# Self-attention of a decoder stack: the softmax is normalised by GpSimd before the transposes, without the matmuls that spread the inverse sums

## The chip, the cores and the metric

One core of a Trainium2 chip runs the whole program. Its engines are TensorE (matmuls and transposes, PE in the rows; PEld are its weight loads), VectorE (DVE), ScalarE (ACT), GpSimd (POOL) and SyncE (SP, which issues DMAs). The metric is the time of the device in microseconds, from the first to the last instruction and what lies around it, the median of several runs.

## The reference, cut to what matters

Two batches of 1024 tokens with 256 features go through two decoder layers. The change is in the first part of all, a self-attention of 16 heads of 64 features with a bias that depends on the distance of two tokens:

```python
x = x + attention(layernorm(x), Wq, Wkv, Wo, bo, rel_emb)      # x: (2, 1024, 256)
# inside, per batch and head:
q, k, v = ...                              # (1024, 64) each
s = q @ k.T * 64 ** -0.5 + bias(rel_emb)   # (1024, 1024)
p = softmax(s, axis=-1)
o = p @ v
```

A cross-attention and a mixture of experts, two attentions within groups, another cross-attention and a low-rank mixture follow. They take the rest of the time and are the same in both kernels.

## The kernel before, in words

The function `self_attention` works through 8 pairs of heads, for each of them through 2 batches, and within these through 8 tiles of 128 queries: 128 iterations n, each with two heads (0 and 1, side by side in the 64-row halves of TensorE). A tile of one head is numbered st = 2n + head; there are 256. For one tile:

- TensorE makes 128x1024 scores in two PSUM banks (L577; a product of float32 is made of three of the rounded parts and their remainders).
- VectorE's `biased` (L734) adds the bias strip, writes the negated sum to one of four buffers `sm` and keeps the row minimum.
- ScalarE's `exps` (L662) makes the exponentials in place and, by its accumulator, their row sums in `rsum`.
- TensorE's `transposed` (L590) turns the 128x1024 exponentials in two halves of four transposes, in two PSUM banks. ScalarE's `emptied` (L667) copies the first bank to `pT`, VectorE's `emptied` (L741) the second.

Two iterations share 256 query columns; such a couple is g = n // 2. One couple later TensorE's `values` (L605) multiplies `pT` by V, one half of the keys in an even iteration and the other in an odd one, into the left half of bank 6. After the second half it makes the **spread** (L612): four small products, each of the inverse sums of one tile, repeated over 64 columns, with the identity. They lay the inverse sum of every query over the 64 rows of its head in the right half of bank 6. ScalarE's `spread_inverse` (L673) copies that half to `inv`, VectorE's `normed` (L752) multiplies the left half by it into `o`, and SyncE stores `o`. VectorE's `inverted` (L746) takes the reciprocal of the four sums of a couple before. So the exponentials are transposed unnormalised, and the output is normalised.

Between these, each of the first 120 iterations projects one unit of the next block's k, q or v (TensorE L628 to L636; ScalarE L683 to L689; VectorE L761 to L768): four units of k and q, then four of v, in turn. The last 8 iterations project nothing.

Each engine runs its own queue in the order in which it is written, and semaphores order the engines: an instruction waits until a count is reached. TensorE's order in iteration n is: scores of n + 1; transposes of head 0 of n; half of the value products of the couple before, with the spread in every second iteration; transposes of head 1 of n; projection. `Signals.zero` (L69 to L71) has GpSimd clear the semaphores of a stage that is over, one instruction for each; in the self-attention that is all that GpSimd does.

Of the kernel before, what the change touches and what calls it, by code (L numbers as in the profile page):

```python
# [28 lines left out]
P = 128  # L29
# [447 lines left out]
def self_attention(nc, A, S, K, psum, early):  # L477
# [6 lines left out]
    with ExitStack() as ctx:  # L484
# [17 lines left out]
        inv = sb("inv", [P, GQ])  # L502
# [25 lines left out]
        with nc.Block() as block:  # L528
# [35 lines left out]
            def _(pe):  # L564
# [17 lines left out]
                def transposed(n, hl):  # L582
                    st = 2 * n + hl
                    pe.wait_ge(sig("exps"), st + 1)
# [8 lines left out]
                def values(g, half):  # L593
# [8 lines left out]
                    for kt in range(half * KT // 2, (half + 1) * KT // 2):  # L602
                        for hl in range(2):
                            rows = slice(hl * DH, (hl + 1) * DH)
                            pe.matmul(bank_o[rows, 0:GQ], V[:, b, kt, rows], pT[:, g % 2, hl, kt, :],  # L605
                                      start=kt == 0, stop=kt == KT - 1)
                    if half:
                        pe.wait_ge(sig("inverse"), g + 1)
                        for t in range(2):
                            for hl in range(2):  # L610
                                at = (4 * g + 2 * t + hl) % SUMS
                                last = pe.matmul(bank_o[hl * DH:(hl + 1) * DH, GQ + t * P:GQ + (t + 1) * P],  # L612
                                                 rsum[:, at:at + 1].broadcast_to([P, DH]), ident[:, :], start=True, stop=True)
# [42 lines left out]
            def _(a):  # L656
                def exps(st):
                    a.wait_ge(sig("biased"), st + 1)
                    at = st % SUMS
                    if st >= SUMS:  # L660
                        a.wait_ge(sig("o_ps"), st // 4 - 2)
# [40 lines left out]
                for n in range(NI):  # L702
                    if n % 2 == 0 and n > 2:
                        spread_inverse(n // 2 - 2)
# [10 lines left out]
                spread_inverse(NG - 2)  # L715
                spread_inverse(NG - 1)

            @block.gpsimd
            def _(g):
                for signals in old:  # L720
                    signals.zero(g)

            @block.vector
            def _(v):
# [18 lines left out]
                def inverted(g):  # L743
                    v.wait_ge(sig("exps"), 4 * (g + 1))
                    part = rsum[:, 4 * g % SUMS:4 * g % SUMS + 4]
                    v.reciprocal(part, part).then_inc(sig("inverse"), 1)  # L746
# [1631 lines left out]
```

## Time and profile before

| | before |
|---|---|
| median of 3 runs | 2372.37 us (2369.58 to 2373.74) |
| the profiled execution | 2370.43 us, its span 2368.7 us |
| granted TensorE clock, mean of the span | 0.943 |
| TensorE busy | 2102.1 us (89% of the span) |
| its weight loads | 1733.0 us (73%) |
| VectorE busy | 1471.8 us (62%) |
| ScalarE busy | 1031.8 us (44%) |
| GpSimd busy | 605.0 us (26%) |
| self-attention's loop | from 54 to 929 us, about |

Busy shares are means over stages with different limits. The page also cuts the span into 40 slices of 59 us: the self-attention is roughly slices 2 to 16, in which TensorE is busy for nine tenths or more, and GpSimd for nothing. Whether an engine waits, and for whom, is read from the timeline and the list of waits. Ends of matmuls are modelled; the starts of weight loads are the firmer mark.

### The profile page before, as it was taken

How to read it: one execution, taken by the hardware profiler on the slowest of the kernel's cores; microseconds unless marked ns; L12 is line 12 of the kernel's file. 1: busy time of each engine (PE TensorE's matmuls, PEld its weight loads, DVE VectorE, ACT ScalarE, POOL GpSimd, SP SyncE). 2: the span in 40 equal slices, each digit the busy share in tenths (PEclk: the TensorE clock that was granted, in tenths of full speed). 3: DMA queues.
4: the chain of work that ended last, by engine and by line, in shares of the span. 5: the costliest groups of instructions: out<-in, count | busy, mean ns of one | idle time of the engine just before them, and what ended most of it. 6: DMA issues, size and time to landing. Idle time of an engine off the chain costs nothing. (4 is left out here: it accounts for less than half of the span.)

```text
span 2368.7 us, 54589 instructions
## 1 busy us (share of the span) xinstructions
PE 2102.1 (89%) x22556; PEld 1733.0 (73%) x22556; DVE 1471.8 (62%) x3140; ACT 1031.8 (44%) x2036; POOL 605.0 (26%) x594
## 2 busy tenths in 40 slices
PE   6999999999999998788887579999868999958885
PEld 4777777777777776667775468999858999956773
DVE  6666666666666664489889645555435454525885
ACT  3666656665666663234333233424224243313442
POOL 1000000000000000166666613343302433424552
PEclk9999999999999999899998779999979999979996
DMA  7001111010101012111200030000021000002000
GB/s 247 15 10 52 43 59 46 17 43 16 46 17 43 12 38 93 56 37 38 65 19 10 18 131 15 12 20 12 11 98 52 29 16 29 12 29 97 10 10 19
DMA packets 59991, 97.17 MB, mean 41 GB/s; under 512 B 7720, under 2 KB 50480, under 8 KB 57392
## 3 DMA queue, kind: packets, MB, share of 16 engines
q1 hardware_dynamic: 53760, 71.98, 9.3%
q10 hardware_dynamic: 5984, 21.69, 2.3%
q8 instruction: 180, 2.95, 0.5%
q14 instruction: 67, 0.55, 0.1%
HBM read 70.45 MB, written 23.20 MB: 40 GB/s over the span
## 5 line engine op out<-in xcount | busy, mean ns | idle before, releaser
L734 DVE CUSTOM_DVE_ANT_0 a_sm<-psum,a_strip 128x1024 f32<-128x1024 f32 x256 | 311.8, 1218 | 33.1 <-PE psum L577 33.1
L662 ACT ACTIVATE a_sm<-a_sm,a_mn 128x1024 f32<-128x1024 f32 x256 | 293.4, 1146 | 29.5 <-DVE a_mn L734 29.4
L667 ACT ACTIVATE a_pT<-psum 128x512 f32<-128x512 f32 x256 | 152.8, 597 | 302.6 <-PE psum L590 302.6
L590 PE MATMUL psum<-ident,a_sm 128*128 128x128 f32 x2048 | 280.0, 280 | 1.1 <-ACT a_pT L667 1.0
L590 PEld LDWEIGHTS psum<-ident,a_sm 128*128 128x128 f32 x2048 | 219.8, 141 | 83.6 <-issue 57.5
L741 DVE COPY a_pT<-psum 128x512 f32<-128x512 f32 x256 | 176.3, 689 | 131.7 <-PE psum L590 131.7
L605 PE MATMUL psum<-a_pT,a_V 128*64 128x256 f32 x2048 | 249.0, 385 | 1.3 <-DVE a_o L752 1.3
L1150 POOL TENSOR_TENSOR b_x_in<-b_x_in,b_bo_a 128x512 f32<-128x512 f32 x8 | 10.2, 1277 | 911.0 <-POOLq L528 911.0
L605 PEld LDWEIGHTS psum<-a_pT,a_V 128*64 128x64 f32 x2048 | 135.7, 136 | 77.7 <-issue 22.1
L1038 PE MATMUL psum<-b_w,b_act_hi 128*128 128x256 f32 x256 | 64.7, 337 | 59.3 <-POOL b_act_lo L1138 59.3
L577 PE MATMUL psum<-a_KH,a_QH 64*128 64x512 f32 x512 | 114.6, 443 | 2.5 <-DVE a_mn L734 2.5
L1146 POOL TENSOR_TENSOR b_gs<-b_gate,b_sg 128x512 f32<-128x512 f32 x64 | 96.6, 1509 | 30.3 <-ACT b_sg L1062 29.8
L577 PE MATMUL psum<-a_KL,a_QH 64*128 64x512 f32 x512 | 101.8, 392 | 0.0
L577 PE MATMUL psum<-a_KH,a_QL 64*128 64x512 f32 x512 | 101.2, 390 | 0.0
L219 PE MATMUL psum<-sa_eT,sa_wqkv 128*128 128x256 f32 x768 | 97.4, 286 | 2.7 <-DVE sa_eT L1777 2.7
L219 PE MATMUL psum<-la_eT,la_wqkv 128*128 128x256 f32 x768 | 97.9, 287 | 1.7 <-DVE la_eT L1777 1.7
L1038 PEld LDWEIGHTS psum<-b_w,b_act_hi 128*128 128x128 f32 x256 | 44.8, 212 | 71.9 <-POOL b_act_lo L1138 70.5
L219 PEld LDWEIGHTS psum<-sa_eT,sa_wqkv 128*128 128x128 f32 x768 | 94.4, 194 | 3.4 <-DVE sa_eT L1777 3.1
L219 PEld LDWEIGHTS psum<-la_eT,la_wqkv 128*128 128x128 f32 x768 | 94.9, 195 | 2.4 <-DVE la_eT L1777 2.1
L1138 POOL TENSOR_TENSOR b_act_lo<-b_act,b_act_hi 128x512 fp32r<-128x512 f32 x64 | 81.7, 1278 | 54.5 <-ACT b_act_hi L1069 54.5
L628 PE MATMUL psum<-a_hT_hi,a_W 128*128 128x512 f32 x256 | 76.5, 421 | 6.8 <-PEq L318 6.8
L1062 ACT ACTIVATE b_sg<-b_gate 128x512 f32<-128x512 f32 x64 | 40.4, 631 | 92.2 <-DVE b_gate L1215 92.0
(379 smaller groups left out, 4584.8 us busy)
## 6 DMA issues: line engine op xcount, KB each, us to landing
a_strip<-table SPq DMA_DIRECT2D x16, 960.0 KB, 6.7
oT<-a_o SPq DMA_DIRECT2D x64, 128.0 KB, 1.9
b_oT_in<-oT SPq DMA_DIRECT2D x8, 1024.0 KB, 5.5
a_raw<-in_a_wqkv SPq DMA_DIRECT2D x7, 384.0 KB, 3.4
s_x<-in_x_rev SPq DMA_DIRECT2D x4, 512.0 KB, 7.5
vb<-s_zero SPq DMA_DIRECT2D x8, 256.0 KB, 2.9
b_x_in<-in_x SPq DMA_DIRECT2D x8, 256.0 KB, 5.6
b_vb_in<-vb SPq DMA_DIRECT2D x8, 256.0 KB, 5.6
```

Of the source, the lines that this page charges most:

```text
L219: last = pe.matmul(bank[:, i * CP:(i + 1) * CP], weight[:, wp, k, m * P:(m + 1) * P], cols[:, cp, k, :], start=n == 0, stop=n == len(terms ...
L577: last = pe.matmul(scores_banks(hl)[:, c, :], qq[rows, b, q], kk[rows, b, k], start=i == 0, stop=i == 2)
L590: last = pe.transpose(psum[:, 4 + j, k * P:(k + 1) * P], sm[:, st % RING, kt * P:(kt + 1) * P], ident[:, :])
L605: pe.matmul(bank_o[rows, 0:GQ], V[:, b, kt, rows], pT[:, g % 2, hl, kt, :], start=kt == 0, stop=kt == KT - 1)
L628: last = pe.matmul(bank, W[:, ws, k, col], hT[hs][:, k, tok], start=i == 0, stop=i == len(terms) - 1)
L662: a.activation(sm[:, st % RING, :], sm[:, st % RING, :], ACT.Exp, scale=-1.0, bias=mn[:, at:at + 1], accum_out=rsum[:, at:at + 1]).then_in ...
L667: a.activation(probs(st, 0), psum[:, 4, :].rearrange("p (k q) -> p k q", k=4), ACT.Copy).then_inc(sig("pT_act"), 1)
L734: v.tensor_tensor_reduce(out=sm[:, st % RING, :], in0=scores_banks(hl).rearrange("p c n -> p (c n)"), in1=strip[:, pair % 2, hl, qt * P:qt ...
L741: v.tensor_copy(probs(st, 1), psum[:, 5, :].rearrange("p (k q) -> p k q", k=4)).then_inc(sig("pT_dve"), 1)
L1038: last = pe.matmul(bank[:, t * D:(t + 1) * D], half[:, e % 2, k, t * P:(t + 1) * P], w2[:, e, k, :], start=i == 0, stop=i == len(parts) - 1)
L1138: g.tensor_tensor(act_lo[:, e % 2, :, :], act[:, e % 2, :, :], act_hi[:, e % 2, :, :].bitcast(F32), ALU.subtract).then_inc(sig("m_lo"), 1)
L1146: g.tensor_tensor(gs[:, n % ER, :, :], gate[:, n % ER, :, :], sg[:, n % ER, :, :], ALU.mult).then_inc(sig("m_gs"), 1)
```

## The change

GpSimd gets work in the self-attention. As soon as the exponentials of a tile and their row sums are there, VectorE takes the reciprocal of that tile's sums (`inverted`, now once a tile), and GpSimd multiplies the whole 128x1024 tile by it, in place (`scaled`), with the reciprocal broadcast along the row as the second operand. TensorE transposes the tile after that. So the exponentials are normalised before they are transposed, and the value products give the output itself: the spread, the copy of it and VectorE's product are gone, and ScalarE copies the output from PSUM to `o` (`stored`). GpSimd clears the old semaphores after its third product.

```diff
                 def transposed(n, hl):
                     st = 2 * n + hl
-                    pe.wait_ge(sig("exps"), st + 1)
+                    pe.wait_ge(sig("scaled"), st + 1)
...
                     if half:
-                        pe.wait_ge(sig("inverse"), g + 1)
-                        for t in range(2):
-                            for hl in range(2):
-                                at = (4 * g + 2 * t + hl) % SUMS
-                                last = pe.matmul(bank_o[hl * DH:(hl + 1) * DH, GQ + t * P:GQ + (t + 1) * P],
-                                                 rsum[:, at:at + 1].broadcast_to([P, DH]), ident[:, :], start=True, stop=True)
                         last.then_inc(sig("o_ps"), 1)
...
-                def spread_inverse(g):
+                def stored(g):
                     a.wait_ge(sig("o_ps"), g + 1)
-                    if g:
-                        a.wait_ge(sig("o_out"), g)
-                    a.activation(inv[:, :], bank_o[:, GQ:2 * GQ], ACT.Copy).then_inc(sig("inv_out"), 1)
+                    if g >= 2:
+                        a.wait_ge(sig(f"st{g % 2}"), 16 * (g // 2))
+                    a.activation(o[:, g % 2, :], bank_o[:, 0:GQ], ACT.Copy).then_inc(sig("o_out"), 1)
...
             def _(g):
-                for signals in old:
-                    signals.zero(g)
+                def scaled(st):
+                    at = st % SUMS
+                    g.wait_ge(sig("inverse"), st + 1)
+                    g.tensor_tensor(sm[:, st % RING, :], sm[:, st % RING, :], rsum[:, at:at + 1].broadcast_to([P, T]),
+                                    ALU.mult).then_inc(sig("scaled"), 1)
+
+                for st in range(2 * NI):
+                    scaled(st)
+                    if st == 2:
+                        for signals in old:
+                            signals.zero(g)
...
-                def normed(g):
-                    v.wait_ge(sig("inv_out"), g + 1)
-                    if g >= 2:
-                        v.wait_ge(sig(f"st{g % 2}"), 16 * (g // 2))
-                    v.tensor_tensor(o[:, g % 2, :], bank_o[:, 0:GQ], inv[:, :], ALU.mult).then_inc(sig("o_out"), 1)
+                def inverted(st):
+                    v.wait_ge(sig("exps"), st + 1)
+                    at = st % SUMS
+                    v.reciprocal(rsum[:, at:at + 1], rsum[:, at:at + 1]).then_inc(sig("inverse"), 1)
...
+                inverted(0)
                 for n in range(NI):
-                    if n % 2 == 0 and n > 2:
-                        normed(n // 2 - 2)
+                    inverted(2 * n + 1)
                     if n and NU + n - 1 < len(units):
                         project(NU + n - 1)
...
                         biased(2 * n + 3)
+                        inverted(2 * n + 2)
                     emptied(2 * n + 1)
-                    if n % 2:
-                        inverted(n // 2)
```

TensorE's queue in an iteration with a spread, from the transposes of head 0 to the next scores, before:

```order
L590 MATMUL psum<-ident,a_sm 128x128 x8
L605 MATMUL psum<-a_pT,a_V 64x256 x8
L612 MATMUL psum<-ident,a_rsum 64x128 x4
L590 MATMUL psum<-ident,a_sm 128x128 x8
L628 MATMUL psum<-a_hT_hi,a_W 128x512 x4
L628 MATMUL psum<-a_hT_lo,a_W 128x512 x2
L577 MATMUL psum<-a_KH,a_QH 128x512 x2
```

and now:

```order
L589 MATMUL psum<-ident,a_sm 128x128 x8
L604 MATMUL psum<-a_pT,a_V 64x256 x8
L589 MATMUL psum<-ident,a_sm 128x128 x8
L621 MATMUL psum<-a_hT_hi,a_W 128x512 x4
L621 MATMUL psum<-a_hT_lo,a_W 128x512 x2
L576 MATMUL psum<-a_KH,a_QH 128x512 x2
```

The spread's four products (L612) are gone; all else stands as it stood.

VectorE's queue from the second half of a projection of k to that of the next one, before (L734 is the bias operation, L761 the projection's second half):

```order
L761 TENSOR_TENSOR a_KL<-psum,a_KH 128x512
L734 ISA a_sm,a_mn<-psum,a_strip 128x1024
L734 ISA a_mn 128x1
L741 COPY a_pT<-psum 128x4x128
L734 ISA a_sm,a_mn<-psum,a_strip 128x1024
L734 ISA a_mn 128x1
L741 COPY a_pT<-psum 128x4x128
L746 RECIPROCAL a_rsum<-a_rsum 128x4
L752 TENSOR_TENSOR a_o<-psum,a_inv 128x256
L761 TENSOR_TENSOR a_KL<-psum,a_KH 128x512
```

and now (L736 is the bias operation, L757 the projection's second half):

```order
L748 RECIPROCAL a_rsum<-a_rsum 128x1
L757 TENSOR_TENSOR a_KL<-psum,a_KH 128x512
L736 ISA a_sm,a_mn<-psum,a_strip 128x1024
L736 ISA a_mn 128x1
L743 COPY a_pT<-psum 128x4x128
L736 ISA a_sm,a_mn<-psum,a_strip 128x1024
L736 ISA a_mn 128x1
L748 RECIPROCAL a_rsum<-a_rsum 128x1
L743 COPY a_pT<-psum 128x4x128
L748 RECIPROCAL a_rsum<-a_rsum 128x1
L757 TENSOR_TENSOR a_KL<-psum,a_KH 128x512
```

The product into `o` and the reciprocal of four sums are gone; a reciprocal of one tile's sums stands ahead of the projection's half and another ahead of the iteration's second copy.

GpSimd's queue where the self-attention begins, before (L71 clears a semaphore, L1150 belongs to the stage after):

```order
L360 MEMSET s_zero 128x512
L318 UNCONDITIONAL_BRANCH
L718 UNCONDITIONAL_BRANCH
L71 ISA x49
L528 UNCONDITIONAL_BRANCH
L1133 UNCONDITIONAL_BRANCH
L1150 TENSOR_TENSOR b_x_in<-b_x_in,b_bo_a 128x512
```

and now:

```order
L360 MEMSET s_zero 128x512
L318 UNCONDITIONAL_BRANCH
L711 UNCONDITIONAL_BRANCH
L716 TENSOR_TENSOR a_sm<-a_sm,a_rsum 128x1024 x3
L71 ISA x49
L716 TENSOR_TENSOR a_sm<-a_sm,a_rsum 128x1024 x253
L527 UNCONDITIONAL_BRANCH
L1126 UNCONDITIONAL_BRANCH
L1143 TENSOR_TENSOR b_x_in<-b_x_in,b_bo_a 128x512
```

The clearing stood first and alone; now it stands behind three products, and 253 follow it.

## Rows read from the trace of the kernel before

**Rows 1.** Stretch table: us and instructions per engine, granted clock, DMA share, GB/s.
```profile
106.00:870.00 764.00, 764.00 (x6121) 564.33 (x6117) 493.74 (x897) 464.08 (x841) 0.00 (x0) 1.00 0.10 33
```

**Rows 2.** List of waits, 100 to 860 us: waiter, releaser; total, times, longest.
```profile
ACT a_pT L667 <- PE psum L590: 266.9, 221, 1.6
```

**Rows 3.** Timeline, two iterations: start, length, engine, line, operation, idle before.
```profile
502.70 1.49 PEld L605 LDWEIGHTS psum<-a_pT,a_V 128*64 128x64 f32 x16 [0.16 <-issue]
...
504.27 0.58 PEld L612 LDWEIGHTS psum<-ident,a_rsum 128*64 128x64 f32 x8
...
504.78 0.08 DVE L734 DVE_READ_ACCUMULATOR2_ANT a_mn<- 128x1 f32 x1
505.02 0.86 PEld L590 LDWEIGHTS psum<-ident,a_sm 128*128 128x128 f32 x8 [0.17 <-issue]
...
507.25 0.19 ACT L662 ACTIVATION_READ_ACCUMULATOR a_sm<-a_sm,a_mn 128x1 f32 x1
...
509.04 0.86 PEld L590 LDWEIGHTS psum<-ident,a_sm 128*128 128x128 f32 x8 [0.37 <-issue]
...
510.06 1.49 PEld L605 LDWEIGHTS psum<-a_pT,a_V 128*64 128x64 f32 x16 [0.16 <-issue]
...
511.94 0.86 PEld L590 LDWEIGHTS psum<-ident,a_sm 128*128 128x128 f32 x8 [0.38 <-ACT a_sm L662]
```

**Rows 4.** Groups of instructions by form, VectorE, 0 to 935 us: busy, mean ns.
```profile
L752 DVE TENSOR_TENSOR a_o<-psum,a_inv 128x256 f32<-128x256 f32 x64 | 27.2, 424 | 78.3 <-ACT a_inv L673 78.3
...
L746 DVE RECIPROCAL a_rsum<-a_rsum 128x4 f32<-128x4 f32 x64 | 10.7, 168 | 0.0
```

**Rows 5.** Groups by form, GpSimd: products with a broadcast second operand.
```profile
L1704 POOL TENSOR_TENSOR la_pr<-la_pr,la_mx 128x512 f32<-128x512 f32 x16 | 16.8, 1050 | 50.8 <-DVE la_mx L1761 50.8
...
L1185 POOL TENSOR_TENSOR b_pr<-b_pr,b_mx 128x256 f32<-128x256 f32 x8 | 5.0, 626 | 20.2 <-DVE b_mx L1317 20.1
```

**Rows 6.** One line's instructions: a GpSimd product of two full operands, ns min/median/max.
```profile
L1146 POOL TENSOR_TENSOR b_gs<-b_gate,b_sg x64: 1265/1486/1845, 1003.1 to 1348.0; 128x512 f32<-128x512 f32 x64
```

**Rows 7.** Timeline, an iteration that projects v.
```profile
93.17 0.08 DVE L734 DVE_READ_ACCUMULATOR2_ANT a_mn<- 128x1 f32 x1
...
96.89 0.86 PEld L590 LDWEIGHTS psum<-ident,a_sm 128*128 128x128 f32 x8 [0.37 <-issue]
```

**Rows 8.** Timeline, an iteration without projection, near the end.
```profile
905.72 0.08 DVE L734 DVE_READ_ACCUMULATOR2_ANT a_mn<- 128x1 f32 x1
...
907.91 0.85 PEld L590 LDWEIGHTS psum<-ident,a_sm 128*128 128x128 f32 x8 [0.36 <-ACT a_sm L662]
```

**Rows 9.** Timeline, the start of the self-attention's loop.
```profile
56.49 0.19 ACT L662 ACTIVATION_READ_ACCUMULATOR a_sm<-a_sm,a_mn 128x1 f32 x1
...
58.18 0.86 PEld L590 LDWEIGHTS psum<-ident,a_sm 128*128 128x128 f32 x8 [0.35 <-ACT a_sm L662]
...
59.59 0.42 PEld L590 LDWEIGHTS psum<-ident,a_sm 128*128 128x128 f32 x4 [0.55 <-issue]
...
65.14 0.42 PEld L590 LDWEIGHTS psum<-ident,a_sm 128*128 128x128 f32 x4 [0.55 <-issue]
```

**Rows 10.** SyncE's waits, 2340 to 2369 us.
```profile
SPq L2258 <- PEq L2258: 4.9, 1, 4.9
```

**Rows 11.** Timeline, the last iterations.
```profile
917.19 0.08 DVE L734 DVE_READ_ACCUMULATOR2_ANT a_mn<- 128x1 f32 x1
...
918.15 0.89 PEld L590 LDWEIGHTS psum<-ident,a_sm 128*128 128x128 f32 x8 [0.55 <-issue]
```

**Rows 12.** Timeline in the stage after: VectorE beside GpSimd.
```profile
1023.08 0.69 DVE L1230 SCALAR_TENSOR_TENSOR b_act<-b_lin,b_gs 128x512 f32<-128x512 f32 x1
...
1025.11 0.88 DVE L1238 SCALAR_TENSOR_TENSOR b_acc<-psum,b_comb,b_acc 128x256 f32<-128x256 f32 x2 [1.34 <-PE psum L1038]
...
1025.35 1.26 POOL L1138 TENSOR_TENSOR b_act_lo<-b_act,b_act_hi 128x512 fp32r<-128x512 f32 x1 [4.10 <-ACT b_act_hi L1069]
...
1025.90 1.26 DVE L1230 SCALAR_TENSOR_TENSOR b_act<-b_lin,b_gs 128x512 f32<-128x512 f32 x1
```

More of the change, by code:

```diff
@@ L501, in self_attention @@
         pT = sb("pT", [P, 2, 2, KT, GQ])
-        inv = sb("inv", [P, GQ])
         o = sb("o", [P, 2, GQ])
@@ L604, in values @@
                             rows = slice(hl * DH, (hl + 1) * DH)
-                            pe.matmul(bank_o[rows, 0:GQ], V[:, b, kt, rows], pT[:, g % 2, hl, kt, :],
-                                      start=kt == 0, stop=kt == KT - 1)
+                            last = pe.matmul(bank_o[rows, 0:GQ], V[:, b, kt, rows], pT[:, g % 2, hl, kt, :],
+                                             start=kt == 0, stop=kt == KT - 1)
                     if half:
-                        pe.wait_ge(sig("inverse"), g + 1)
-                        for t in range(2):
-                            for hl in range(2):
-                                at = (4 * g + 2 * t + hl) % SUMS
-                                last = pe.matmul(bank_o[hl * DH:(hl + 1) * DH, GQ + t * P:GQ + (t + 1) * P],
-                                                 rsum[:, at:at + 1].broadcast_to([P, DH]), ident[:, :], start=True, stop=True)
                         last.then_inc(sig("o_ps"), 1)
@@ L660, in exps @@
                     if st >= SUMS:
-                        a.wait_ge(sig("o_ps"), st // 4 - 2)
+                        a.wait_ge(sig("scaled"), st - SUMS + 1)
                     a.activation(sm[:, st % RING, :], sm[:, st % RING, :], ACT.Exp, scale=-1.0,
@@ L703, in _ @@
                     if n % 2 == 0 and n > 2:
-                        spread_inverse(n // 2 - 2)
+                        stored(n // 2 - 2)
                     emptied(2 * n)
@@ L714, in _ @@
                         split(n // (2 * KT) + 1)
-                spread_inverse(NG - 2)
-                spread_inverse(NG - 1)
+                stored(NG - 2)
+                stored(NG - 1)
             @block.gpsimd
             def _(g):
-                for signals in old:
-                    signals.zero(g)
+                def scaled(st):
[8 more added lines that the diff above has]
+                            signals.zero(g)
             @block.vector
@@ L741, in emptied @@
                     v.tensor_copy(probs(st, 1), psum[:, 5, :].rearrange("p (k q) -> p k q", k=4)).then_inc(sig("pT_dve"), 1)
[L743 to L746, printed above, removed]
-                def normed(g):
-                    v.wait_ge(sig("inv_out"), g + 1)
-                    if g >= 2:
-                        v.wait_ge(sig(f"st{g % 2}"), 16 * (g // 2))
-                    v.tensor_tensor(o[:, g % 2, :], bank_o[:, 0:GQ], inv[:, :], ALU.mult).then_inc(sig("o_out"), 1)
+                def inverted(st):
+                    v.wait_ge(sig("exps"), st + 1)
+                    at = st % SUMS
+                    v.reciprocal(rsum[:, at:at + 1], rsum[:, at:at + 1]).then_inc(sig("inverse"), 1)
                 def project(u):
@@ L789, in _ @@
                         biased(2 * n + 3)
+                        inverted(2 * n + 2)
                     emptied(2 * n + 1)
-                    if n % 2:
-                        inverted(n // 2)
                     if n % (2 * KT) == 3 and n // (2 * KT) + 1 < HP:
                         split(n // (2 * KT) + 1)
-                normed(NG - 2)
-                normed(NG - 1)
     for signals in old:
```

## The prediction

> **What bounds the kernel now.** The change touches the self-attention alone, so I first asked which engine sets the pace there. The stretch table of its steady part [rows 1] shows the reader TensorE busy for all of 764.00 us at a granted clock of 1.00 (the upper of its two levels, 2.4 GHz); VectorE is busy 493.74, ScalarE 464.08, GpSimd 0.00. The list of waits says the same from the other side: ScalarE waited 266.9 us for transposes of TensorE [rows 2]. So an instruction taken from TensorE's queue there shortens the stage by its slot, as long as nothing that TensorE needs comes later than the shortened queue asks for it.
>
> The timeline of two neighbouring iterations [rows 3] shows the slot. In the first, the weight loads of the value products end at 502.70 + 1.49 = 504.19; then come the spread's own (504.27, 0.58 us long), and the next transposes start at 505.02: 0.83 us after the value products. In the second, without a spread, they start at 511.94, which is 0.39 after 510.06 + 1.49 = 511.55. The difference, 0.44 us, is what a spread costs TensorE. The row at 511.94 names an exponential of ScalarE as releaser. By the code these transposes need the one that ended at 507.25 + 0.19 = 507.44; the named one is the next pair's, so this is a coincidence of times, and the 0.39 is the queue's own.
>
> **What the change removes.** (a) 64 spreads, one per two query tiles. 63 stand in the running queue: 63 x 0.44 = 27.7 us. The last stands alone at the end: about its 0.58 us of loads [rows 3]. (b) 64 normalising products of VectorE of 424 ns [rows 4] and the copy of the inverse sums on ScalarE, in whose place a copy of the output of the same shape stands. Both lie beside TensorE; only the last ones show, one VectorE product at the very end (0.42), and some 0.4 (my allowance, of the same size) where the last value products waited for the one before it.
>
> **What it adds: a longer way from exponential to transpose.** Each of the 256 tiles now goes exponential, reciprocal, GpSimd product of 128x1024, transposes. The reciprocal of four sums takes 168 ns [rows 4]; for one I take the same. The product does not occur in this trace. Nearest is a product with a broadcast second operand, the same form: 626 ns at 256 columns and 1050 at 512 [rows 5], that is 1.66 ns a column, so 1050 + 512 x 1.66 = 1.90 us at 1024. From above, a product of two full operands takes at least 1265 ns at 512 [rows 6], so twice that, 2.53 us. Below 1.90 I would not go: one half of it is measured at 1.05. I take 1.90, since its rows have the same kind of operand, and keep 2.53 for the range. With 0.1 us (my allowance) for each of two signals between engines the way is 0.17 + 1.90 + 0.2 = 2.3 us longer (2.9 at the upper end).
>
> The Trainium skill (GPSIMD Engine Reference, "Elementwise — side-by-side cycle accounting") speaks against the change: GpSimd needs about 2.6 cycles an element where both operands are tensors, since its two read streams share a port, and its table has 4497 ns for 2048 columns; half of that would be an estimate of 2.25 us. The full-operand rows of this case are in line with such a rate, the broadcast rows are quicker; at 2.25 the sum below would come out some 4 us later.
>
> Is there room? Head 0, projecting q or k [rows 3]: the reciprocal follows the second bias operation (504.78 + 0.08 = 504.86), the product ends at 504.86 + 2.3 = 507.1 (507.8), and the transposes start at 509.04, after the change at 508.6. Spare 1.5 us (0.8). Projecting v [rows 7]: 93.17 + 0.08 + 2.3 = 95.5 (96.2) against 96.89 - 0.44 = 96.45; spare 0.9 (0.3). Head 1: the exponential ends at 507.44, the product at 509.7 (510.3) against 511.94 [rows 3]; spare 2.2. GpSimd's two products take 3.8 (5.1) of an iteration of 6.77 us on average. So in 120 of 128 iterations nothing is late. The 8 last iterations have no projection: 905.72 + 0.08 + 2.3 = 908.1 (908.7) against transposes at 907.91 [rows 8]: 0.2 (0.8) late where the wait falls in an iteration without spread, about the same in the other after the shortening. Two kinds, some 1 us together at 1.90, up to 6 at 2.53.
>
> The reciprocals wait in VectorE's queue, one for the second head at the top of an iteration, one for the first head between the second bias operation and a copy. Behind the first stands the second half of a projection, which waits for a ScalarE instruction issued after that same exponential anyway; behind the second, a copy that sits idle for TensorE. 256 reciprocals of 0.17 replace 64 of 0.17 and 64 products of 0.42: 43 us in place of 38, hidden in VectorE's idle time, 1 - 493.74 / 764.00 = 35%. SyncE's stores now wait for ScalarE's copy, which comes earlier than VectorE's product did. Of the stage's start, the first product ends at 56.49 + 0.19 + 2.3 = 59.0 against transposes at 58.18, the second a product later, 60.9 against 59.59 [rows 9]: 1.3 us late. Then GpSimd clears 49 semaphores, after its third product. The trace has one wait that holds such a clearing, of the block that ends the program, 4.9 us [rows 10]; I take that as the upper end and nothing as the lower. The fourth product ends between 60.9 + 2 x 1.9 = 64.7 and 69.6, and its transposes would stand at 65.14 + 1.3 = 66.4 [rows 9]: 0 to 3.2 us late, I take 1.7, the middle. Start: 3.0 us in all; 1.3 at least, and at 2.53 a product with the full clearing 7. At the stage's end the last head-0 product ends at 917.19 + 0.08 + 2.3 = 919.6 against 918.15 [rows 11], 1.4 late, of which a missing spread gives 0.44 back; less the 0.4, 0.58 and 0.42 of above: -0.5.
>
> **The sum.** -27.7 + 3.0 + 1 - 0.5 = -24.2 us. The profiled execution took 2370.4 (span 2368.7), the median of the runs is 2.0 above it; 2372.4 - 24.2 = 2348. With the kind values -27.7 + 1.3 - 0.5 = -26.9: 2345.5; with the unkind ones -27.7 + 7 + 6 - 0 = -15: 2357.
>
> **Does GpSimd disturb VectorE?** In the later stage where both work, a VectorE operation on PSUM and one SBUF tensor takes 0.88 for two across the start of a GpSimd product, which takes 1.26, as that product does at its shortest; one that reads two SBUF tensors takes 1.26 instead of 0.69 and ends only 0.55 after that product [rows 12]. In the self-attention the bias operation, the copies and the projections read PSUM and at most one SBUF tensor; with two there is only the splitting of weights, 7 times. So I count no contention. The Trainium skill (SBUF — State Buffer, "SBUF: two separate sides") says that the pair of ports the two engines share is an exclusive lock, taken by VectorE with two SBUF inputs; the trace agrees.
>
> **Rivals.** (1) The product is at its upper bound and the start is slow: 2357, still faster. For it: full-operand rows. Against: broadcast rows. (2) The bias operation, a custom one, is held up by GpSimd after all: its product for head 1 would run from 507.7 to 509.6, just when VectorE finishes a projection and starts the next bias operation (which the transposes at 509.04 follow in TensorE's queue) [rows 3]. VectorE's idle time, 35% of 6.77 us, is 2.4 an iteration, so not all of a hold reaches TensorE; I price half a product, 0.95, in every second iteration: 64 x 0.95 = 61 us on top of the forecast, 2409, slower than before. From 24.2 / 64 = 0.38 on it decides. For it: no row shows this custom operation beside a working GpSimd. Against: rows 12, where a PSUM operand kept the other one out. (3) GpSimd becomes the pace: 256 products must fit into the 918.15 - 58.18 = 860 us between the first transposes and the last pair's [rows 9, 11], 6.77 an iteration; from 3.36 us on (1.68 for 512 columns) it is slower than before. The longest product of 512 columns took 1845 ns [rows 6]; twice that is 3.69, 256 x 3.69 = 945, +85: 2457. Against: that one has two full operands and stands in a stage with two-SBUF operations on VectorE. (4) The freed slot is filled by another wait of TensorE, on the copies that empty the transposes' banks; then nothing is gained, 2372. Against: it is the copies that wait for TensorE [rows 2].
>
> **How the numbers follow.** Forecast 0.76, rival (1) 0.12, (2) 0.05, (3) 0.04, (4) 0.03. Of the forecast and rival (1) nearly all lies between 2343 and 2360, which is the range: the kind end less 2 us of scatter, the unkind end plus 3. About what a measurement tells from no change is 0.2%, 5 us. Faster 0.88, within it 0.03, slower 0.09.
>
> **What would show it.** Right: the gap before head 1's transposes is 0.38 in every iteration; GpSimd's 256 products take 1.9 us each; TensorE still is busy for all of the steady part; the stage from the first transposes to the last pair's is 26 us or so shorter. Wrong: transposes that wait for GpSimd there; bias operations well over 1.22 us; products over 2.9 us; a granted clock under 1.00.

## The result and the profile after

| | before | after |
|---|---|---|
| first four executions of each, median | 2370.97 us | 2340.9 us (2339.0 to 2349.21) |
| ratio, with its 95% interval | | 0.9881 (0.9853 to 0.9909) |
| all executions of this study, mean | 2372.3 (33) | 2343.6 (13) |
| profiled execution, span | 2368.7 us | 2337.2 us |
| granted clock, mean of the span | 0.943 | 0.941 |

The change makes the kernel faster, by 30.1 us in the first medians and by 28.7 (twice the standard error is 2.3) over all executions. 24.2 was forecast: 2348, with 2343 as the lower end. The sign and the mechanism were right, the size too small and the range too narrow below. Luck has a part in how far it missed: the mean of all 13 executions, 2343.6, lies just inside the range, their median, 2342.6, just outside.

The stretch table of the steady part, after (columns as in [rows 1]):

```profile
106.00:840.00 734.00, 734.00 (x5631) 531.51 (x5628) 499.80 (x1001) 461.54 (x834) 417.80 (x221) 1.00 0.10 34
```

TensorE is still busy all the time at a granted clock of 1.00, and GpSimd now works for 57% of it. Groups of instructions of the self-attention, after (busy us and mean ns of one behind the bar, then the idle time before them and what ended it):

```profile
L716 POOL TENSOR_TENSOR a_sm<-a_sm,a_rsum 128x1024 f32<-128x1024 f32 x256 | 485.3, 1896 | 390.0 <-DVE a_rsum L748 388.0 <-issue 2.0
L736 DVE CUSTOM_DVE_ANT_0 a_sm<-psum,a_strip 128x1024 f32<-128x1024 f32 x256 | 312.2, 1220 | 57.8 <-PE psum L576 57.8
...
L748 DVE RECIPROCAL a_rsum<-a_rsum 128x1 f32<-128x1 f32 x256 | 41.2, 161 | 76.6 <-ACT a_sm L655 76.6
...
L769 DVE TENSOR_TENSOR a_W<-a_raw,a_W 128x768 fp32r<-128x768 f32 x7 | 9.9, 1410 | 0.0
```

GpSimd's product takes 1896 ns, the 1.90 that the broadcast rows gave [rows 5]. The bias operation (L736) is as before, 1220 against 1218 ns. The last row is the one VectorE operation of the loop with two SBUF inputs, the splitting of weights: 1410 ns a piece, 927 in the profile of before.

The timeline of two neighbouring iterations that project k, after; it answers to [rows 3]:

```profile
483.92 1.49 PEld L604 LDWEIGHTS psum<-a_pT,a_V 128*64 128x64 f32 x16 [0.16 <-issue]
...
485.80 0.86 PEld L589 LDWEIGHTS psum<-ident,a_sm 128*128 128x128 f32 x8 [0.39 <-issue]
...
490.82 1.49 PEld L604 LDWEIGHTS psum<-a_pT,a_V 128*64 128x64 f32 x16 [0.17 <-issue]
...
492.69 0.86 PEld L589 LDWEIGHTS psum<-ident,a_sm 128*128 128x128 f32 x8 [0.39 <-issue]
...
492.90 0.16 DVE L748 RECIPROCAL a_rsum<-a_rsum 128x1 f32<-128x1 f32 x1
493.14 1.90 POOL L716 TENSOR_TENSOR a_sm<-a_sm,a_rsum 128x1024 f32<-128x1024 f32 x1 [2.75 <-DVE a_rsum L748]
...
495.15 0.16 DVE L748 RECIPROCAL a_rsum<-a_rsum 128x1 f32<-128x1 f32 x1 [0.63 <-ACT a_sm L655]
...
495.39 1.90 POOL L716 TENSOR_TENSOR a_sm<-a_sm,a_rsum 128x1024 f32<-128x1024 f32 x1 [0.36 <-DVE a_rsum L748]
...
496.71 0.86 PEld L589 LDWEIGHTS psum<-ident,a_sm 128*128 128x128 f32 x8 [0.37 <-issue]
...
499.61 0.86 PEld L589 LDWEIGHTS psum<-ident,a_sm 128*128 128x128 f32 x8 [0.38 <-issue]
```

The transposes of head 1 start 0.39 and 0.38 us after the loads of the value products (483.92 + 1.49 = 485.41 to 485.80, and 492.31 to 492.69) in the two iterations; the 0.83 of every second one is gone. Head 0's product ends at 493.14 + 1.90 = 495.04 and TensorE wants it at 496.71: 1.67 us to spare. Head 1's ends at 497.29 for 499.61: 2.3 to spare. Both are near the 1.5 and 2.2 of the prediction, and neither transpose row names GpSimd as what it waited for. The list of waits from 100 to 840 us has no wait of TensorE for GpSimd at all.

Two iterations without projection, after, as [rows 8]:

```profile
869.45 1.90 POOL L716 TENSOR_TENSOR a_sm<-a_sm,a_rsum 128x1024 f32<-128x1024 f32 x1 [1.36 <-DVE a_rsum L748]
...
871.63 0.86 PEld L589 LDWEIGHTS psum<-ident,a_sm 128*128 128x128 f32 x8 [0.36 <-POOL a_sm L716]
...
875.32 3.81 POOL L716 TENSOR_TENSOR a_sm<-a_sm,a_rsum 128x1024 f32<-128x1024 f32 x2 [1.73 <-DVE a_rsum L748]
...
877.27 0.86 PEld L589 LDWEIGHTS psum<-ident,a_sm 128*128 128x128 f32 x8 [0.49 <-POOL a_sm L716]
```

The first product ends at 871.35, in time for 871.63: the 0.36 is the queue's own gap, although the row names GpSimd. The second row of GpSimd holds two products; the first of them ends near 877.2, and TensorE starts at 877.27 with 0.49 of idle time, 0.13 more than its own gap. Of head 0's transposes in the 8 last iterations these are the only sizes, 0.36 and once 0.49, but for the last pair, which follows below.

The start of the loop, after, as [rows 9]:

```profile
58.42 0.86 PEld L589 LDWEIGHTS psum<-ident,a_sm 128*128 128x128 f32 x8 [1.07 <-POOL a_sm L716]
...
60.27 0.86 PEld L589 LDWEIGHTS psum<-ident,a_sm 128*128 128x128 f32 x8 [1.00 <-POOL a_sm L716]
...
61.53 1.90 POOL L716 TENSOR_TENSOR a_sm<-a_sm,a_rsum 128x1024 f32<-128x1024 f32 x1 [1.32 <-DVE a_rsum L748]
...
65.39 1.89 POOL L716 TENSOR_TENSOR a_sm<-a_sm,a_rsum 128x1024 f32<-128x1024 f32 x1 [1.96 <-issue]
...
67.33 0.86 PEld L589 LDWEIGHTS psum<-ident,a_sm 128*128 128x128 f32 x8 [2.19 <-POOL a_sm L716]
```

The first transposes start 4.73 us after the first bias operation (53.69 in this profile), before 58.18 - 54.17 = 4.01: 0.72 late. Between the third product's end, 63.43, and the fourth's start lie 1.96 us of "issue": the clearing of the 49 semaphores. The fourth pair's transposes start 67.33 - 58.42 = 8.91 after the first, before 65.14 - 58.18 = 6.96: 1.95 late. The end, after, as [rows 11]:

```profile
891.21 0.86 PEld L589 LDWEIGHTS psum<-ident,a_sm 128*128 128x128 f32 x8 [0.39 <-issue]
...
891.65 1.89 POOL L716 TENSOR_TENSOR a_sm<-a_sm,a_rsum 128x1024 f32<-128x1024 f32 x1 [1.38 <-DVE a_rsum L748]
...
893.59 0.86 PEld L589 LDWEIGHTS psum<-ident,a_sm 128*128 128x128 f32 x8 [1.53 <-POOL a_sm L716]
...
898.39 3.25 PEld L604 LDWEIGHTS psum<-a_pT,a_V 128*64 128x64 f32 x32 [1.04 <-ACT a_pT L660]
...
904.91 0.38 SPq L799 DMA_DIRECT2D b_oT_in<-oT  x1
```

The last pair waits 1.53 us for its product. From the last value products (898.39) to the next stage's first load (904.91) it takes 6.52 us. Before, they started here:

```profile
923.87 3.25 PEld L605 LDWEIGHTS psum<-a_pT,a_V 128*64 128x64 f32 x32 [1.48 <-issue]
```

and the next stage's load was issued at 931.27: 7.40 us.

Put together, in us, each from marks in the two profiles:

| part | before | after | change | forecast |
|---|---|---|---|---|
| up to the first bias operation | 54.17 | 53.69 | -0.5 | 0 |
| first bias operation to first transposes | 4.01 | 4.73 | +0.7 | +0.8 |
| first transposes to the last value products | 865.69 | 839.97 | -25.7 | -27.7 + 2.2 + 1, and +0.5 |
| last value products to the next stage | 7.40 | 6.52 | -0.9 | -1.0 |
| self-attention, sum | 877.10 | 851.22 | -25.9 | -24.2 |
| all after it | 1437.4 | 1432.3 | -5.1 | 0 |

The two spans differ by 31.5 us, 7.3 more than was forecast: 1.7 us of this lie in the self-attention and 5.6 outside it, where no instruction was changed. What lies behind it differs in its first part: the cross-attention and the first mixture of experts took 437.5 us before and 432.1 after.

### The profile page after: what moved, and what is told of

It is laid out like the page before. It is cut to its first block and busy times, and to the rows that moved or that the text cites. A ratio compares the mean times of both kernels' runs of the same rounds, so it can differ in the third digit from the quotient of the medians.

```text
span 2337.2 us, 53886 instructions
## 1 busy us (share of the span) xinstructions
PE 2074.3 (89%) x22044; PEld 1699.6 (73%) x22044; DVE 1479.1 (63%) x3268; ACT 1032.9 (44%) x2036; POOL 1092.2 (47%) x850
## 5 line engine op out<-in xcount | busy, mean ns | idle before, releaser
L716 POOL TENSOR_TENSOR a_sm<-a_sm,a_rsum 128x1024 f32<-128x1024 f32 x256 | 485.3, 1896 | 390.0 <-DVE a_rsum L748 388.0
L736 DVE CUSTOM_DVE_ANT_0 a_sm<-psum,a_strip 128x1024 f32<-128x1024 f32 x256 | 312.2, 1220 | 57.8 <-PE psum L576 57.8
L748 DVE RECIPROCAL a_rsum<-a_rsum 128x1 f32<-128x1 f32 x256 | 41.2, 161 | 76.6 <-ACT a_sm L655 76.6
```

What stands on the lines that cost most here:

```text
L716: g.tensor_tensor(sm[:, st % RING, :], sm[:, st % RING, :], rsum[:, at:at + 1].broadcast_to([P, T]), ALU.mult).then_inc(sig("scaled"), 1)
L736: v.tensor_tensor_reduce(out=sm[:, st % RING, :], in0=scores_banks(hl).rearrange("p c n -> p (c n)"), in1=strip[:, pair % 2, hl, qt * P:qt ...
```

## The experiments

Twelve runs, of eight new kernels and again of the changed one, each beside executions of the kernel before. "Loop" is the distance from the first transposes to the last value products in its profile.

| kernel | executions | mean, us | against before (2372.3) | loop, us |
|---|---|---|---|---|
| before | 33 | 2372.3 | | 865.69 |
| changed | 13 | 2343.6 | -28.7 +- 2.3 | 839.97 |
| before, without spreads | 8 | 2340.6 | -31.7 +- 2.8 | 838.10 |
| before, with products beside | 10 | 2371.7 | -0.6 +- 2.5 | 865.68 |
| both of these | 4 | 2341.6 | -30.7 +- 3.7 | 838.09 |
| changed, cleared last | 8 | 2341.7 | -30.6 +- 1.9 | 838.57 |
| changed, full operand | 4 | 2343.4 | -28.9 +- 4.3 | 842.11 |
| changed, 3 copies of delay | 4 | 2347.6 | -24.7 +- 2.7 | 840.22 |
| changed, 5 copies of delay | 4 | 2349.0 | -23.3 +- 3.7 | 841.53 |
| changed, two products a tile | 2 | 2487.8 | +115.5 +- 3.7 | 986.23 |

The +- are twice the standard error. The executions come from four groups, three of them on three different chips, whose own means for the kernel before were 2370.8, 2371.2, 2374.3 and 2373.1 us. Against those of its own group the changed kernel gained 28.3, 32.3 and 27.4 us, the two kernels with copies of delay 26.7 and 25.3, and the one with two products lost 113.5. So a us or two in the differences of the table can come from the groups.

Loops agree within 0.3 us between profiles of one kernel, unless TensorE's clock falls for a moment in the loop's start: in the second profile of the changed kernel the granted clock from 69 to 73 us was 0.57, and the loop took 841.62. The same happened with full operand (0.58 from 61 to 65 us) and with 5 copies of delay (0.72 from 66 to 72 us).

**Without the spreads (e1_nospread).** What a spread costs TensorE, alone.

```diff
...
                         pe.wait_ge(sig("inverse"), g + 1)
-                        for t in range(2):
+                        for t in range(0 if g else 2):
...
```

> The kernel before, with the four spread matmuls left out in 63 of 64 couples (the inverse sums are spread once, for the first couple; so the outputs are scaled by wrong sums). Nothing is added on GpSimd. Slot theory: TensorE's gap before head 1's transposes falls from 0.83 to 0.38 in every second iteration; the stage from the first transposes to the last pair's is 27.7 us shorter (62 to 63 x 0.44), so some -28 in the self-attention and at its end, and the rest of the program is the same within the scatter of the clock, +-5. Rival (the slot is refilled by a wait for ScalarE's or VectorE's copies): under 10 us shorter. Rival (the stages after it become shorter by the change itself, not by chance): those keep their 1437 us here, since GpSimd is as before.

The timeline of its first transposes and its last value products:

```profile
58.63 0.91 PEld L590 LDWEIGHTS psum<-ident,a_sm 128*128 128x128 f32 x8 [0.65 <-issue]
...
896.73 3.25 PEld L605 LDWEIGHTS psum<-a_pT,a_V 128*64 128x64 f32 x32 [1.48 <-issue]
```

The loop is 838.10 us, 27.6 shorter than before; with the 62 spreads inside it that is 0.445 each. The slot theory holds, the refilled slot is out (under 10 was its mark). In its profile all that follows took 1440.5 us, not less than before. The first transposes start 5.3 us after the first bias operation here, not 4.0 as before: the granted clock was 0.66 from 55 to 60 us. Six more of these profiles show such a fall just ahead of the loop; it shifts the loop and lengthens it by 0.3 us at most.

**With products beside (e2_beside).** Whether GpSimd's work disturbs VectorE.

```diff
...
+                g.memset(aside[:, :], 1.0).then_inc(sig("beside"), 1)
+                for st in range(2 * NI):
+                    g.wait_ge(sig("exps"), st + 1)
+                    g.wait_ge(sig("beside"), st + 1)
+                    g.tensor_tensor(aside[:, :], aside[:, :], mhalf[:, 0:1].broadcast_to([P, T]),
+                                    ALU.mult).then_inc(sig("beside"), 1)
```

> The kernel before, with 256 GpSimd products of 128x1024 by a broadcast operand added beside the work: each waits for an exponential as a signal, works on a buffer of its own, and nobody waits for it. No-contention theory (two SBUF inputs on VectorE are the only thing that collides): the bias operation stays at 1.22 us, its copies at 0.69, only the seven weight splits grow from 0.93 to some 1.4 us, and the self-attention keeps its length, 0 +-1 us. Contention theory: bias operations of 1.5 us and more, and the stage 20 to 60 us longer.

The groups of the kernel with products beside (columns as above; L727 is the product that nobody reads, L780 the weight splits):

```profile
L727 POOL TENSOR_TENSOR a_aside<-a_aside,mhalf 128x1024 f32<-128x1024 f32 x256 | 485.8, 1898 | 391.3 <-ACT a_sm L663 390.8
L741 DVE CUSTOM_DVE_ANT_0 a_sm<-psum,a_strip 128x1024 f32<-128x1024 f32 x256 | 311.7, 1218 | 34.3 <-PE psum L578 34.3
...
L748 DVE COPY a_pT<-psum 128x512 f32<-128x512 f32 x256 | 176.3, 689 | 131.8 <-PE psum L591 131.8
...
L780 DVE TENSOR_TENSOR a_W<-a_raw,a_W 128x768 fp32r<-128x768 f32 x7 | 6.5, 927 | 0.0
```

The bias operation and the copies take what they took, and the loop is the same to 0.01 us (865.68 against 865.69). Rival (2) of the prediction is out, for this custom operation too.

A part of the expectation failed: the weight splits stayed at 927 ns. The timeline tells why. One split in the changed kernel:

```profile
187.93 1.90 POOL L716 TENSOR_TENSOR a_sm<-a_sm,a_rsum 128x1024 f32<-128x1024 f32 x1 [2.75 <-DVE a_rsum L748]
189.22 1.41 DVE L769 TENSOR_TENSOR a_W<-a_raw,a_W 128x768 fp32r<-128x768 f32 x1
```

and one here:

```profile
192.66 0.93 DVE L780 TENSOR_TENSOR a_W<-a_raw,a_W 128x768 fp32r<-128x768 f32 x1
193.34 2.01 POOL L727 TENSOR_TENSOR a_aside<-a_aside,mhalf 128x1024 f32<-128x1024 f32 x1 [1.14 <-ACT a_sm L663]
```

In the changed kernel the split starts 0.61 us before a product ends (189.83) and ends 0.80 after it. Here the split starts first and keeps its 0.93 us, and the product that starts beside it takes 2.01 us in place of 1.90. Whichever of the two began first kept its time, and the other one took longer.

**Both (e11_nospread_beside).** Everything that the change takes and adds, but nobody waits for GpSimd.

```diff
...
-                        for t in range(2):
+                        for t in range(0 if g else 2):
...
+                    g.tensor_tensor(aside[:, :], aside[:, :], mhalf[:, 0:1].broadcast_to([P, T]),
+                                    ALU.mult).then_inc(sig("beside"), 1)
...
```

> The kernel before without 63 of 64 spreads and with 256 GpSimd products beside the work that nobody waits for: everything that the change takes and adds, except that TensorE waits for GpSimd. Slot theory: the self-attention as in the kernel without spreads, 850 to 852 us; the product costs nothing. The difference from the changed kernel's loop (832.79 us from the first transposes to the last but one pair's) is the whole price of the longer way: 2 us at the start and next to nothing at the end. If GpSimd's activity makes the rest shorter, its mean is 2 to 3 us below that of the kernel without spreads and without products.

Its loop is 838.09 us. The changed kernel's is 839.97, so the price of the longer way in the loop is 1.9 us, or 2.3 with the first spread (0.445), which this kernel keeps and the changed one has not. The starts of VectorE's bias operations tell where it lies: from the 13th to the 245th it takes 769.06 us in this kernel (90.74 to 859.80) and 769.06 in the changed one (91.75 to 860.81). So these 116 iterations lose nothing, and the price is paid in the start (1.7 us with the first spread) and at the last pair (0.6). No sign that GpSimd's work shortens the rest: 1440.5 us in its profile.

**Cleared last (e3_clearlast, and again e12_clearlast_again).**

```diff
                 for st in range(2 * NI):
                     scaled(st)
-                    if st == 2:
-                        for signals in old:
-                            signals.zero(g)
+                for signals in old:
+                    signals.zero(g)
```

> The changed kernel, with the 49 semaphores cleared after GpSimd's last product in place of after its third. Start theory: the clearing took the 1.96 us between third and fourth product, so the fourth pair of transposes (at 67.33) comes 1.9 us earlier and the self-attention is 1.9 us shorter; at the end the clearing is hidden behind the last value products. Rival: the start's other waits (copies, ScalarE) fill it, 0 to -0.5. The whole time can hide it: the clock of the stages after scatters by +-5 us.

The start of its loop in the timeline:

```profile
58.15 0.86 PEld L589 LDWEIGHTS psum<-ident,a_sm 128*128 128x128 f32 x8 [1.08 <-POOL a_sm L716]
...
61.27 3.75 POOL L716 TENSOR_TENSOR a_sm<-a_sm,a_rsum 128x1024 f32<-128x1024 f32 x2 [1.32 <-DVE a_rsum L747]
...
65.41 0.42 PEld L589 LDWEIGHTS psum<-ident,a_sm 128*128 128x128 f32 x4 [0.55 <-POOL a_sm L716]
```

The third and fourth product now follow each other (61.27 for 3.75 us), and the fourth pair's transposes start 65.41 - 58.15 = 7.26 after the first in place of 8.91. The loop is 838.57, 1.4 shorter than the changed kernel's, not 1.9: of the 1.95 us 0.3 were the longer way without the clearing, and some 0.2 come back behind. Once more:

> The changed kernel with the clearing behind the last product, a second time, since its gain (1.9 us in the loop's start) is smaller than the scatter of a few executions. The mean is 1 to 2.5 us below the changed kernel's in this call; the distance from the first transposes to the last but one pair's is 1.9 us shorter than the changed kernel's in executions whose clock does not fall in it.

Loop 838.42 us, in a profile whose clock fell just ahead of the loop; the changed kernel's third profile, with the same fall, has 840.22, so the gain is 1.8 us there. Over 8 executions its mean is 2341.7, 1.9 below the changed kernel's, with an uncertainty of 2.5: in line, but the time alone doesn't show it; the loops do. Of the versions that leave nothing out it has the shortest loop.

**A full second operand (e4_fulloperand).** A slower product, by its operand.

```diff
...
-                    g.tensor_tensor(sm[:, st % RING, :], sm[:, st % RING, :], rsum[:, at:at + 1].broadcast_to([P, T]),
+                    g.tensor_tensor(sm[:, st % RING, :], sm[:, st % RING, :], full[:, :],
...
+                g.memset(full[:, :], 0.001).then_inc(sig("full"), 1)
+                g.wait_ge(sig("full"), 1)
...
```

> The changed kernel, with a full 128x1024 constant tile as second operand of each product (so the exponentials are scaled by a constant in place of the inverse sums). From the full-operand rows (1265 ns at 512) a product takes 2.4 to 2.53 us in place of 1.90. Slack theory (spare 0.9 us in a v iteration, 1.5 in a k or q one): 120 iterations do not change; the 8 without projection lose some 0.5 each, the start and the end 0.5 to 1 per product on their path: +4 to +8 us in the self-attention. Rival (GpSimd's time is already on TensorE's path): 128 x 0.5 = +64 and more.

The product (L717) and the weight splits (L772) among its groups:

```profile
L717 POOL TENSOR_TENSOR a_sm<-a_sm,a_full 128x1024 f32<-128x1024 f32 x256 | 606.7, 2390 | 250.2 <-DVE a_rsum L751 248.4 <-issue 1.5
...
L772 DVE TENSOR_TENSOR a_W<-a_raw,a_W 128x768 fp32r<-128x768 f32 x7 | 13.4, 1911 | 0.0
```

A product takes 2390 ns, 0.49 us more, and the loop grows by 2.1 us. The starts of the bias operations show where: 0.8 up to the 13th, in a start with a fall of the clock, so that the product's own part of it stays open; nothing from the 13th to the 245th (769.09 us, changed 769.06); 1.3 from there on, in the iterations without projection and at the last pair. So 256 x 0.49 = 126 us of GpSimd time cost 2 at most: the slack is real, and the expectation of 4 to 8 was too high. The weight splits now take 1911 ns: one starts 1.09 us before its product ends and ends 0.82 after it.

**Two products a tile (e8_double).** Where GpSimd becomes the pace.

```diff
...
+                    g.tensor_tensor(sm[:, st % RING, :], sm[:, st % RING, :], K["mhalf"][:, 0:1].broadcast_to([P, T]),
+                                    ALU.mult).then_inc(sig("once"), 1)
+                    g.wait_ge(sig("once"), st + 1)
...
```

> The changed kernel with two GpSimd products per tile (the first by the constant -0.5 broadcast, so the outputs are scaled), one after the other: 2 x 1.9 = 3.8 us a tile. The prediction put the point from which GpSimd sets the pace at 3.36 us a tile (860 us over 256). Pace theory: the loop takes 256 x (3.8 + 0.1 to 0.35 between products) = 998 to 1060 us in place of 835, so the kernel 160 to 230 us more than the changed one, and TensorE waits for GpSimd in every iteration. Rival (TensorE still paces, GpSimd is only late at the start and the end): +15 us.

TensorE's waits for the second product between 100 and 980 us (us in all, times, longest):

```profile
PEld psum L589 <- POOL a_sm L719: 205.1, 229, 1.3
```

One tile in its timeline:

```profile
501.60 1.90 POOL L716 TENSOR_TENSOR a_sm<-a_sm,mhalf 128x1024 f32<-128x1024 f32 x1
...
503.58 1.90 POOL L719 TENSOR_TENSOR a_sm<-a_sm,a_rsum 128x1024 f32<-128x1024 f32 x1
...
505.43 1.90 POOL L716 TENSOR_TENSOR a_sm<-a_sm,mhalf 128x1024 f32<-128x1024 f32 x1
505.52 0.86 PEld L589 LDWEIGHTS psum<-ident,a_sm 128*128 128x128 f32 x8 [1.12 <-POOL a_sm L719]
```

This tile takes 505.43 - 501.60 = 3.83 us of GpSimd; on average it is 3.85 (the first product of the first tile starts at 56.86, of the last at 1039.34, 255 tiles later). TensorE waited for it 229 times in this stretch, 205.1 us in all. The self-attention takes 999.5 us in this profile, 122.4 more than before. With 256 us more for each us a tile, before's time is reached at 3.85 - 122.4 / 256 = 3.37 us; the prediction had 3.36. The expected 160 to 230 us over the changed kernel were too many (it is 144), as was the loop of 998 to 1060 (it is 986): 0.1 to 0.35 us had been allowed between products, and the rows above have 0.08 between the two of a tile and nothing behind the second.

**Again, and delayed (e5_again, e9_again, e10_nospread_again, e6_delay3, e7_delay5).** What moves the rest, that is all that follows the self-attention. The delay, with three copies (the other kernel has `range(5)`):

```diff
...
                 stored(NG - 2)
                 stored(NG - 1)
+                for i in range(3):
+                    a.wait_ge(sig("o_out"), NG + i)
+                    a.activation(sm[:, 0, :], sm[:, 1, :], ACT.Copy).then_inc(sig("o_out"), 1)
...
```

> The changed kernel again, unchanged, for more executions of it and a second profile. The self-attention took 877.10 us before and 851.22 after (-25.9), but the medians of all runs differ by 29.5. Scatter theory: outside the self-attention nothing changed; the mixture stage (431.6 us before, 426.2 after, 434.8 in the kernel without spreads) just meets the falls of TensorE's clock differently in every execution, so more runs move the median toward 2370.4 - 25.9 = 2344.5, and the new profile's mixture stage lies anywhere from 426 to 435. Systematic theory: the stages after it are some 3 us shorter by the change; the median stays at 2341 and the mixture stage at 426 to 428.

> The changed kernel a third time. So far: its 8 executions have a mean of 2342.3, those of the kernel before 2372.0 (24 executions), a difference of 29.8 of which the self-attention in the traces explains 24 to 26. The profiles show that what lies behind the self-attention (1429 to 1442 us over nine kernels) follows the time that TensorE's clock spent at its lower level. Scatter theory: the new executions come out at 2344 to 2346 on average and the one profile's rest anywhere from 1429 to 1442. Systematic theory (the clock falls less by the change): 2342 again, the rest at 1429 to 1434.

> The kernel before without 63 of 64 spreads, a second time (outputs scaled by wrong sums). Self-attention 850 to 852. If what changes the rest is only that the later stages begin 26 us earlier, or nothing at all, this kernel's mean equals that of the changed kernel within 1.5 us. If it is GpSimd's work or the changed order of waits, this one's is 2 to 4 us longer: its first four executions had a mean of 2343.0.

> The changed kernel with three chained ScalarE copies of 128x1024 behind its last store copy: they end the self-attention about 902.5 + 3 x 1.25 = 906.3 in place of 904.8, some 1.6 us later. Scatter theory: the median rises by about 1.6 us and the length of the mixture stage does not follow the delay. Rival (the mixture stage's length depends on the moment at which it begins after the start of the program): the median moves by several us against that, either way, and the mixture stage with it, in all runs alike.

> The same with five copies, some 4.2 us later. Scatter theory: +4 us, the mixture stage between 426 and 435. Rival (dependence on the moment): it differs from the kernel with three copies by several us beyond the 2.6 us of added delay, in all runs alike.

All that follows the self-attention, in the profiles: changed kernel 1432.3, 1434.0, 1435.2; cleared last 1432.8, 1437.4; full operand 1428.9; two products 1430.7; delayed 1441.6, 1440.8; without spreads 1440.5, 1437.9; both 1440.5; before 1437.4; before with products beside 1440.0. The instructions are the same in all of them. The stretch table of what follows, of the changed kernel (columns as in [rows 1]):

```profile
905.00:2337.00 1432.00, 1196.77 (x15408) 1066.18 (x15408) 870.96 (x2016) 484.49 (x1044) 597.44 (x576) 0.91 0.12 38
```

and of the one with 3 copies of delay:

```profile
907.00:2348.00 1441.00, 1200.76 (x15408) 1069.90 (x15408) 874.23 (x2016) 483.61 (x1044) 595.30 (x576) 0.90 0.12 38
```

The second takes 9 us more for the same 15408 matmuls and 2016 VectorE instructions, at a granted clock of 0.90 in place of 0.91. Over the 14 profiles the length goes with the time that the clock spent at its lower level (254 to 282 us), but loosely (correlation 0.52). The two profiles above spent 265 and 278 us there; at half the clock, 13 us more are 7 of the 9 us at most. So the clock's falls can be a part of the scatter and not all of it.

The two repeats moved opposite ways: the changed kernel's five new executions had a mean of 2345.7, the four of the kernel without spreads 2338.1. From the last value products to the next stage's first load it took 7.64 us with three copies and 9.83 with five, where the changed kernel has 6.52: delays of 1.1 and 3.3 us. The two kernels are 5.6 and 7.0 us above the changed one's executions of their group (uncertain by 3.5 and 4.3), so some 4 us more than their delays, and their rests are the longest two of all. That the length of the rest depends on the moment at which it begins is not excluded.

The systematic theory in its sharp form (2341 to 2342 again, the rest at 1429 to 1434) is refuted by the third profile and its executions, the scatter theory not proved in full: 28.7 less the 25.9 of the self-attention leaves 2.8 +- 2.3 us, the kernels without spreads leave some 3.7 of 31.7, as their self-attention is 28.0 shorter. GpSimd's work is not what they have in common. An earlier start of the later stages is, but it alone doesn't explain it: with two products a tile these stages start 122 us later than before, and took 1430.7 us in place of 1437.4. Whether these 3 us are an effect or luck stays open.

## Why the prediction was wrong, point by point

- **TensorE sets the pace; a spread costs 0.44 us.** Right: 27.6 us for 62 of them without anything else changed, 0.445 each.
- **The product takes 1.90 us.** Right, 1.896. The rate by the rows of the same form of operand was the one to take; a full operand takes 2.39.
- **Head 0 has 1.5 us to spare (0.9 projecting v), head 1 2.2; 120 iterations lose nothing.** Right: 1.67 (1.1: 853.95 for 855.09) and 2.3, no transposes wait for GpSimd there, and the pace from the 13th to the 245th bias operation is that of the kernel in which nobody waits for it.
- **The 8 last iterations: +1.** Too much: 0.13 once and nothing otherwise, the last pair aside. I had allowed 0.1 for each signal and counted the queue's own gap of 0.36 as if it came after the product; it runs beside it.
- **The start: 3.0.** 0.7 + 1.95 = 2.7 at the fourth pair, 2.4 behind it; the clearing's unknown price was 1.96 us between products, where 0 to 4.9 stood.
- **The end: -0.5.** -0.88 behind the last value products and +0.64 in the end of the loop, so -0.2. Between the last pairs it lost 1.0 (transposes 2.38 after the pair before in place of 1.40) and won 0.4, the wait for VectorE's product. The 0.44 of a missing spread was taken twice in the prediction: it is among the 63, and in the profile of before no spread stands between the last scores (912.27) and these transposes (918.15). That the product came 1.0 late and not 1.4 hid it.
- **No contention.** Right for the bias operation, and for the copies with products beside. The weight splits do take 0.48 us more each; TensorE's pace doesn't show it.
- **The failing step is a term that the sum put at nothing: all that lies outside the self-attention.** The sum for the self-attention itself was 1.7 us short (24.2 for 25.9). Of its terms, the spreads gave 28.0 in place of 27.7, the start cost 2.4 in place of 3.0 and the last iterations nothing in place of 1, and the end gave 0.3 less. The kind end was -26.9, 2345.5, and the self-attention came out inside it. For the rest the prediction had 0 in the sum and 2 us of scatter in the range, and the two profiles differ by 5.6 us there. The same instructions behind the self-attention took 1429 to 1442 us in the 14 profiles, and the executions of one kernel spread over 10 us and more (2365.0 to 2377.5 before). By this spread a median of four carries some 2 us either way (my estimate), and over all executions a remainder of 2.8 +- 2.3 us lies outside the changed stage; its cause stays open. The three executions of before (2369.6 to 2373.7) showed only a part of this spread, and I took it for the whole.
- **Rivals.** (1) is out (full operand: +2 us, not +9), (2) is out (the same loop to 0.01 us), (3) has the right threshold (3.37 for 3.36) and doesn't apply at 1.90, (4) is out.

## What to carry to other kernels

An instruction group in the queue of an engine that never waits is worth the distance of its neighbours with it less that without it, read at two like places: 0.44 us here, and 0.445 measured. Work moved to an idle engine, in the way between two others, costs nothing in the steady part until its latency exceeds the spare time of the tightest iteration or its total the engine's pace; both are worked out from one iteration's rows, with the duration from rows of the same operand form. And a range needs the scatter of the stages that are not touched: with 1430 us behind the change in which the clock rises and falls, four executions tell 2 us at best (an estimate from the spread above).

## What the runs showed of the hardware

- GpSimd multiplies 128x1024 by a broadcast column in 1.90 us and by a full tile in 2.39 us.
- 49 semaphores cleared by GpSimd in a row took 1.96 us, 40 ns each.
- A VectorE operation with two SBUF inputs that started while a GpSimd product ran ended 0.80 us after that product: it took 1410 ns in place of 927, and 1911 beside the longer products. In [rows 12] the end was 0.55 us after. Where it started before the product it kept its 927 ns, and the product took 2.01 us in place of 1.90. An operation with PSUM and one SBUF input took 1220 ns in place of 1218.
- The granted clock can fall for a moment in the first iterations. In the changed kernel's second profile TensorE had waited 2.6 us for the fourth product; from 69 to 73 us the granted clock was then 0.57, and the loop 1.7 us longer (841.62 for 839.97). In the first profile TensorE waited 2.2 us at the same place and the clock stayed at 1.00.
